# Loads of x and stores of the result issued from ScalarE's DMA queue in a fused cross-attention and feed-forward kernel

## The reference, cut to what matters

```python
x = x + xattn(layernorm(x), ctx_1024, ctx_1024, mask, Wq, Wk, Wv, wq_h, ..., Wo)   # one head of 16, tiled
x = x + ffn(layernorm(x), w1, b1, w2, b2)     # 256 -> 1024, gelu, 1024 -> 256

def ffn(x, w1, b1, w2, b2):
    h = gelu(einsum('bsd,hd->bsh', x, binarize(w1)) + b1)
    return einsum('bsh,dh->bsd', h, binarize(w2)) + b2
```

## Time and profile before

| what | value |
|---|---|
| time, median of 3 runs | 333.26 us (332.15 to 333.83) |
| time of the profiled execution | 331.71 us |
| its span, first to last instruction | 329.9 us |
| mean granted TensorE clock | 0.95 |
| busy share of PE, DVE, ACT, POOL | 90%, 87%, 79%, 75% |
| DMA traffic | 40.33 MB; queue of SP 39.90 MB, queue of ACT 0.05 MB |

### The profile page before, as it was taken

One profiled execution on the slowest core, in us unless ns is written; L12 is line 12 of the kernel. 1 busy time (PEld: TensorE's weight loads), 2 busy tenths in 40 slices (PEclk: granted clock), 3 DMA queues, 4 the chain that ended last, 5 costly groups with the idle time before them and its releaser, 6 DMA issues.

```text
span 329.9 us, 6163 instructions
## 1 busy us (share of the span) xinstructions
PE 297.6 (90%) x2055; PEld 201.5 (61%) x2055; DVE 285.9 (87%) x637; ACT 261.3 (79%) x330; POOL 247.9 (75%) x412
## 2 busy tenths in 40 slices
PE   1999999598989898989899989898989899999994
PEld 1735666265657575757576657575666666676673
DVE  0999996999999999999998999999999796976444
ACT  1079553799898989898989798989899989788770
POOL 2480608695999999999999999999999857668331
PEclk9995755999999999999999999999999999999998
DMA  7957668283547493839474747473535425251311
GB/s 238 329 203 156 75 104 112 63 171 64 127 66 201 69 194 69 195 74 193 80 193 80 193 80 194 80 192 71 138 66 143 67 79 67 78 130 30 100 64 64
DMA packets 85183, 40.33 MB, mean 122 GB/s; under 512 B 77464, under 2 KB 80672, under 8 KB 85152
## 3 DMA queue, kind: packets, MB, share of 16 engines
q1 hardware_dynamic: 84240, 39.90, 53.6%
q10 hardware_dynamic: 912, 0.05, 0.2%
HBM read 12.80 MB, written 8.39 MB: 64 GB/s over the span
## 4 chain that ended last, share of the span: by engine, by line
PE 40%; POOL 28%; DVE 13%; DMA 8%; issue 6%; ACT 5%; SPq 0%; POOLq 0%; DVEq 0%; ACTq 0%
PE psY L1336 17%; PE psZ L1351 16%; POOL xh L458 8%; DMA xT_lo<-w_sb 6%; POOL x1b L482 4%; POOL w_sb L493 4%; POOL rstd L447 4%; POOL sc L469 3%; PE psY L1239 3%; DVE st_raw L717 3%; PE psW L1312 2%; DMA x_in<-in_x 2%; POOL vare L442 2%; PE psW L1292 2%; ACT psY L579 1%
## 5 line engine op out<-in xcount | busy, mean ns | idle before, releaser
L1351 PE MATMUL psZ<-sgn2T,h_hi 128*128 128x256 f16 x512 | 115.2, 273 | 0.0
L1351 PE MATMUL psZ<-sgn2T,h_lo 128*128 128x256 f16 x512 | 115.2, 273 | 0.0
L1336 PE MATMUL psY<-xT_hi,sgn1T 128*128 128x512 f16 x256 | 97.0, 379 | 15.3 <-DMA xT_lo<-w_sb 12.2
L579 ACT ACTIVATE psY<-psY,b_col,alpha1x 128x512 f32<-128x512 f32 x128 | 93.5, 750 | 12.4 <-PE psY L1336 9.6
L839 DVE SCALAR_TENSOR_TENSOR h_lo<-psY,h_scale,h_hi 128x1024 f16<-128x1024 f32 x64 | 81.2, 1269 | 18.8 <-ACT h_hi L588 18.8
L1336 PE MATMUL psY<-xT_lo,sgn1T 128*128 128x512 f16 x256 | 97.0, 379 | 0.0
L588 ACT ACTIVATE h_hi<-psY,h_scale 128x1024 f16<-128x1024 f32 x64 | 71.2, 1113 | 4.5
L493 POOL TENSOR_TENSOR w_sb<-w_sb,x1b 128x256 f32<-128x256 f32 x62 | 47.1, 791 | 14.3 <-DVE w_sb L853 14.3
L1351 PEld LDWEIGHTS psZ<-sgn2T,h_hi 128*128 128x128 f16 x512 | 50.1, 98 | 9.7 <-DVE h_lo L839 0.2
L1351 PEld LDWEIGHTS psZ<-sgn2T,h_lo 128*128 128x128 f16 x512 | 50.1, 98 | 9.5
L1336 PEld LDWEIGHTS psY<-xT_hi,sgn1T 128*128 128x128 f16 x256 | 25.0, 98 | 43.1 <-issue 16.1
(11 more groups left out here) (145 smaller groups left out, 449.3 us busy)
## 6 DMA issues: line engine op xcount, KB each, us to landing
out_x<-w_sb SPq DMA_DIRECT2D x15, 512.0 KB, 3.1
x_in<-in_x SPq DMA_DIRECT2D x6, 512.0 KB, 4.2
ctx_sb<-in_x SPq DMA_DIRECT2D x6, 512.0 KB, 4.2
w_sb<-in_L_ffn_w SPq DMA_DIRECT2D x2, 1024.0 KB, 8.2
wkq<-in_x SPq DMA_DIRECT2D x4, 512.0 KB, 4.1
ctx_sb<-in_ctx SPq DMA_DIRECT2D x1, 1024.0 KB, 6.0
out_x<-w_sb SPq DMA_DIRECT2D x2, 256.0 KB, 2.1
wkq<-in_L_xattn_Wk SPq DMA_DIRECT2D x1, 256.0 KB, 7.2
```

Of the source, the lines that this page charges most:

```text
L579: nc.scalar.activation(y, y, ACT.Gelu, bias=b1_col[:, c:c + 1], scale=alpha1x[:, c:c + 1]).then_inc(gelu_done, 1)
L1336: last = nc.tensor.matmul(psY[q % 2][:, c % 2, :], sgn1T[:, c, k, :], part[b % 2][:, :, k, :], start=(n == 0), stop=(n == 2 * KD - 1))
L1351: last = nc.tensor.matmul(Z[n][:, (j % 2) * D:(j % 2 + 1) * D].rearrange("p (k t) -> p k t", k=KD), part[q][:, u, j * P:(j + 1) * P], sgn2 ...
```

## The change

`load_x` and `store` for the steps are issued by ACT in place of SP. On SP the calls in `step` go, the loads of the prologue stay. On ACT `load_x(b + 5)` stands after `round_e(b + 2)` and `store(b - 2)` after `round_h(b - 1, 2)`. The transfers, their sizes, their buffers and the semaphores that they wait for and raise are the same.

```diff
             def step(b):                       # SP
-                load_x(b + 5)
                 turn_hi(b, 1)
                 turn_lo(b, 1)
                 turn_e(b + 2)
                 turn_hi(b + 4, 0)
-                store(b - 2)
                 turn_lo(b + 4, 0)
...
+            def load_x(b):                     # ACT
+                if absent(b):
+                    return
...
+                wait(act, x1_ready, val(b - NX, 2, 2))
+                act.dma_start(x_in[b % NX], x_v[b, :, :, :]).then_inc(x_loaded[b % NX], 16)
+
+            def store(b):                      # ACT
+                if absent(b):
+                    return
+                if b == B - 1:
+                    for n in range(2):
+                        act.wait_ge((out_ready, out_half_ready)[n], (B, 1)[n])
+                        act.dma_start(out_v[b, :, 2 * n:2 * n + 2, :], z_sb[b % 2][:, 2 * n:2 * n + 2, :]) \
+                          .then_inc(out_stored[b % 2], 16)
+                    return
+                act.wait_ge(out_ready, val(b, 1, 1))
+                act.dma_start(out_v[b, :, :, :], z_sb[b % 2]).then_inc(out_stored[b % 2], 16)
...
                 gelu(b - 1, 4)                 # ACT, in step(b)
                 gelu(b - 1, 5)
                 round_e(b + 2)
+                load_x(b + 5)
                 round_h(b - 1, 2)
+                store(b - 2)
                 gelu(b - 1, 6)
                 gelu(b - 1, 7)
                 round_h(b - 1, 3)
```

More of the change, by code:

```diff
@@ L343, in turn_sign_2 @@
                              transpose=True).then_inc(sgn2T_ready, 16)
[L345 to L355, removed]
             def load_w(dst, src, name):
@@ L521, in _ @@
                 act.dma_start(dst, src.rearrange("(p a) -> p a", a=1)).then_inc(loaded["biases"], 16)
+            def load_x(b):
+                if absent(b):
+                    return
+                if b == 2 or b == 3:
+                    act.wait_ge(pe_ctxT, 4)
+                elif b == 4 or b == 5:
+                    act.wait_ge(pe_kq_heads, 1)
+                wait(act, x1_ready, val(b - NX, 2, 2))
[11 more added lines that the diff above has]
+                act.dma_start(out_v[b, :, :, :], z_sb[b % 2]).then_inc(out_stored[b % 2], 16)
             def copy_turned(n):
```

## The result

| | before | after |
|---|---|---|
| median, lowest to highest | 332.76 us (332.15 to 333.83) | 345.26 us (343.64 to 345.94) |
| runs | 4 | 4 |
| profiled execution, its span | 331.71, 329.9 us | 344.70, 342.9 us |
| mean granted TensorE clock | 0.95 | 0.93 |

After over before is 1.035 (95% interval 1.031 to 1.040), and the medians differ by 12.5 us. Executions more than 1.5% above the fastest of the same kernel are left out of all times and ratios here, except where they are named. The forecast was 335.4 us in a range up to 340.5. Its sign was right and its size was not.

A forecast was written before the change was run, and what follows sets the result against it. Bound: rings of engines waiting for each other, the longest through ACT, DVE and POOL at 16.92 us a step. Removal, issues and tail cost nothing; the delayed turn adds 2.1 us to 333.26: 335.4 us, range 332.3 to 340.5.

The forecast's parts named there:

- removal from SP: Taking load and store issues off SP's queue gains nothing, since SP waits for ACT and DVE before each turn.
- the issues on ACT: Load beside `round_x`, store behind gelu 5: both issues are covered by ACT's work and cost nothing.
- Rival 2: ACT's queue doesn't run ahead of a DMA issue; load and store cost some 0.7 us each a step: 347 us, chance 0.05.
- Rival 3: On ACT, the store's issue waits for the turn's, making gelu 6 late by 0.65 us a step: 340 us, chance 0.08.
- ring two: Loop from `round_x` through DVE's split, SP's turn, PE and ACT: 16.04 us, 0.88 us under the period.
- d: How much later `turn_lo(b, 1)` lands because the store's data moves beside it: taken as 1.3 us.
- The estimate of 0.65 us: The turn's delay if DMA engines share by whole packets, letting in about half of the store.
- one for one: SP's and ACT's queues pass packets alternately whatever their size, so the turn lands later by the whole store, 1.3 us.
- e: Lengthening of the step's period by the late turn: 0.21 us a step, times 10 steps, 2.1 us.
- without that help: If DVE's split does not move earlier with POOL: 0.42 us a step, 4.2 us in all.
- Tail. Nothing.: In the last steps ACT's 0.9 us lateness at gelu 6 is made good, and the last store's waits are unchanged: no cost.
- ring one: Loop from ACT's `round_x` through `round_h`, DVE and POOL back to ACT: 16.92 us, setting the period before the change.

The follow-up runs named there:

- stores alone: The changed kernel with only the stores issued by ACT, the loads staying on SP: 341.81 us beside 334.55 for the kernel before, ratio 1.025.
- the three partial kernels: The changed kernel with the store at the changed place only in steps 2 to 4, 5 to 10 or 11 to 17: 339.05, 338.51, 338.69 us; before 333.66.
- loads alone: The changed kernel with only the loads of x issued by ACT, the stores staying on SP: 335.7 us beside 334.55 before, ratio 1.003.
- small transfers: The kernel before with two added 2 KB transfers a step, issued by ACT at the change's two places: 334.92 us, ratio 1.000.
- half store: The changed kernel with ACT issuing only 256 KB of each store, SP the other half in its old place: 335.6 us beside 334.96 before, ratio 1.002.
- the early store: The changed kernel with load and store moved ahead of `round_e`: four executions took 345.27, 354.76, 357.7 and 339.63 us.
- more data: The changed kernel with ACT loading another 256 KB behind each store into an unread buffer: 361.68 us beside 334.96 before, ratio 1.082.

## Why the prediction was right in kind and wrong in size

**Right: removal from SP gains nothing.** With the store out of the turns' way (at the end of the step) the time is the same, 0.998.

**Right: the issues on ACT cost nothing.** ACT's queue runs ahead of its datapath over a DMA issue too: the load's issue lies inside `round_x`, the store's ends 0.73 us before gelu 6 starts. They are shorter than thought, 0.33 to 0.37 us against 0.57 to 0.64. Rival 2 forecast 347 us, close to the number measured, by a mechanism that the runs exclude: small issues at both places cost 0.000 (-0.002 to +0.003). Rival 3 is out for the same reason; the store's issue ran within the turn's.

**Right: the store's data delays the turn, and ring two takes over.** d was taken as 1.3 us and is 1.44 in step 9 (4.50 - 3.06). The Trainium skill, DMA: Bandwidth & Descriptors, section Issuing engines are not separate DMA queues, says that transfers of all issuing engines share the same 16 DMA engines and that a second one saves only issue time; the trace agrees, with 120 packets of ACT's queue at 108% of those engines. Its section Queues, rings and completion order has the engines turn between queues packet by packet. The estimate of 0.65 us that the forecast made from it is not borne out: the turn landed 1.44 us later. Whether the page is wrong here is open. 217.6 to 220.6 us shows one transfer nearly whole before the other, but if nine of the profile's packets an engine are one of the page's packets, the page has it so; and at 0.27 us the two did mix. The forecast's one for one is not what step 9 shows either.

**Wrong: "I take it that it moves with POOL, and the turn starts earlier by e."** This was to halve the loss, 0.21 us a step. In step 9 POOL's residual starts 0.14 us before `round_x` (212.67 against 212.81) and did so by 0.13 us before; SP issues the turn 3.81 us after `round_x` starts, in both. The timelines of DVE and POOL in the changed kernel show why:

```profile
214.97 1.57 DVE L759 SCALAR_TENSOR_TENSOR w_sb<-xh,w_sb 128x1024 f16<-128x1024 f32 x1
...
224.11 1.40 DVE L759 SCALAR_TENSOR_TENSOR ctxT<-xh,ctxT 128x1024 f16<-128x1024 f32 x1 [0.38 <-ACT ctxT L553]
225.43 0.36 DVE L739 BATCH_NORM_AGGREGATE st<-st_raw 128x2 f32<-128x6 f32 x4
```

```profile
225.88 0.20 POOL L428 TENSOR_SCALAR vare<-st 128x4 f32<-128x4 f32 x1 [1.46 <-DVE st L739]
```

The split itself became shorter, 1.57 instead of 1.86 us, as assumed. But DVE came to it 2.16 us behind the start of `round_x`, 1.88 in the earlier trace rows, and the two cancel. POOL can't get ahead of ACT: its next `norm` waits for DVE's statistics, which stand behind a split that waits for ACT's `round_x(b + 4, 0)`, which stands behind `gelu(b, 0)`, the first instruction that the late turn delays. So e = d - 0.88 without help: 0.56 us in step 9 against 0.47 measured (the way from `gelu(b, 0)` to the next `round_x` is 7.93 us, 0.09 less than before without its wait). Over ten steps it is 4.2 us where 2.1 was forecast, the "without that help" figure of the working.

The signs named ahead: landing 4.31 to 4.50 us in ten of the steps 2 to 12 and 5.19 in step 4 (4.2 to 4.4 forecast), period 17.39 (17.1 to 17.3), PE's wait 15.9 / 9 = 1.8 us (2.0 or more), ACT's idle time before `round_x` gone and POOL waiting, as forecast.

**Wrong: "Tail. Nothing."** The working looked only at whether ACT's gelu 6 would be late there, and that was right: ACT stands 0.61 us for POOL in step 15, and no time is lost by it. It did not look at the turn in the tail. There the steps have less work (16.0, 15.3 and 14.1 us before) and with it ring one goes, and its slack of 0.88 us: PE sets the pace, and a stand of PE is lost whole. The chain, first before and then after:

```profile
275.39 3.50 DMA xT_lo<-w_sb
...
278.98 1.89 PE psY L1336 x8
280.87 1.75 PE psZ L1351 x16
```

```profile
284.93 5.25 DMA xT_lo<-w_sb
...
290.27 3.27 PE psY L1348 x8
293.53 2.05 PE psZ L1363 x16
```

After this turn the chain is PE without a gap in both kernels. So the tail's 4.3 us are: 0.8 before the turn's issue, 1.75 in its landing, and 1.7 in the matmuls behind it, where the clock had fallen again.

This store was issued at 286.13, 1.20 us behind the turn, and yet the two met. The DMA view has one packet of instructions, 16 KB, at 284.5 to 284.9 us, in the middle of `turn_hi`'s data; behind it, from 285.4 to 286.0, only 19 packets of SP's queue start. `turn_hi` landed after 3.99 us, the issue of `turn_lo` took 1.65 us instead of 1.23, and its last packets moved behind the store's. DMA view, 289.0 to 289.7 us:

```profile
q10 hardware_dynamic: 53, 0.15, 53.8%
q1 hardware_dynamic: 32, 0.00, 2.6%
```

The kernel before has such a packet there too (its turn landed after 3.50 us), but no store behind it. That the packet delays the turn is read from the order in time and was not tried.

**Left out: the clock.** The working took every wait of PE at its length. In this case a wait can cost more. Between 75 and 320 us the granted clock fell in the changed kernel, in stores alone, and in the three partial kernels, six times in all, each time just behind a stand of PE of 2.06 to 2.97 us. In the kernels where PE's longest stand there was 1.90 us or less (before, loads alone, small transfers, store at the end, half store, store 1.35 us later) it never fell. It doesn't follow every long stand: four others, of 2.04 to 2.90 us, had none behind them. The repeat of the changed kernel, the early store and more data have ten falls more, at stands of 2.06 to 3.88 us, and five stands of 2.00 to 2.55 us without one. The forecast expected PE to wait "2.0 us or more a step" and so had the condition in hand, though not its price. Two falls at 1.7 us are 3.4 of the 13 us.

The Trainium skill, TensorE: Matmul & The Clock Gate, Part 1, says that TensorE drops from 2.4 to 1.2 GHz when it has been idle and gets the full rate back after sustained work; the trace agrees in that a PE stand came before each fall, and it would have been a rule to weigh.

**Probably not the change's: 1.7 us at step 1.** In the profiled execution after, the low clock of the prologue lasted from 24 to 65 us without a break, before and with the store at the end it was broken (24 to 37 and 41 to 58 us). The prologue's program is the same in the changed kernel and in the one with the store at the end, of which one profiled execution had the 1.7 us and the other 0.10. Of the fourteen profiled executions three have the short form (before, store at the end, half store), and eleven are 1.4 to 1.8 us later at step 1; loads alone, small transfers and the store 1.35 us later are among these, with ratios of 1.000 to 1.003. The profiled execution of before lay 1.05 us under the median of its four runs, which fits a prologue that more often has the longer form.

In sum, beside those 1.7 us: ten steps 4.2 instead of 2.1, step 4 to 5 with its fall 2.8 instead of 0.2, the tail 4.3 instead of 0, that is 11.3 us in the profiled executions. The medians differ by 12.5; 1.2 us of that are not placed. The turn of step 4 (127.31) landed after 5.19 us instead of 4.4, and after 5.16 and 5.40 us in two other kernels. In its data, too, stands a packet of instructions (8 KB, in the DMA view of 130.9 to 131.9 us), and from 131.3 to 131.8 us only 18 packets of SP's queue start. That this is the cause was not tried. What decides which long stand is followed by a fall stays open.

## What to carry to other kernels

Moving a transfer to another queue moves its data in time, and that matters more than the issue: look for the transfer that somebody waits for, and keep large ones from starting before its data has moved. Here one placed 1.25 us later cost nothing, and one 0.2 to 0.8 us behind delayed the turn more than one just beside it. The distance of the issues is no guarantee: in the tail a store 1.20 us behind met a turn that had itself been held up. When a wait grows past its slack, follow the loop all the way round before letting another engine's slack pay it back, and do it again for the tail, where the loop that gave the slack may be gone. Where the wait is TensorE's, price it with the clock behind it.

## What the runs showed of the hardware

- Two transfers issued 0.1 us apart on two queues did not share the engines evenly: the plain store of 512 KB went nearly whole (120 of 144 packets in 1.4 us) ahead of the transpose that had been issued first. With the store 0.27 us behind they mixed, and the transpose landed later still (4.86 us); with the store 1.35 us behind, the transpose went first (3.09 us).
- An issue on ACT's queue took 0.33 to 0.37 us amid work, less than the 0.57 us on SP's, and delayed no ACT instruction.
- Between a load, a store and two transposes, an issue of a transpose took 2.36 us instead of 1.23, and one landed after 7.13 us.
- A fall of the granted clock in mid-kernel lasted about 3.4 us ((1 - 0.57) x 2 x 4.00 us in the windows above) and cost about 1.7 us of matmul time.
